# A post-LN decoder layer on one core: the gated attention stage with fp32 scores on 32-row groups, turned values and new orders

## The chip, the cores and the metric

One Trainium2 chip, one of its cores. The time is the device time of one launch in microseconds, as the median of several runs. Engines: TensorE (PE in the profile, PEld for its weight loads), VectorE (DVE), ScalarE (ACT), GpSimd (POOL) and SyncE (SP), which issues the transfers. The program is written instruction by instruction: each engine has its own list and runs it in order, and the lists are tied by semaphores.

## What is computed

Eight sequences of 128 tokens and 256 channels run through three sublayers, each followed by a layer norm of x + f(x).

```
x = layernorm(x + attention(x, Wq, Wk, Wv, Wo))      # 16 heads of 128, 4 key groups, RoPE
x = layernorm(x + convmix(ctx, ctx, x, kernel, D))   # long convolution of k*v, times x
x = layernorm(x + gated(x, W_gate, W_qkv))

def gated(x):
    gating = softmax(x @ W_gate.T)                   # 16 heads
    indicator, top1 = one_hot(argmax(gating)), max(gating)
    q, k, v = split(x @ W_qkv.T)                     # each 16 heads of 16
    k_shared = sum_h indicator * k                   # one key of 16 for a token
    v_shared = sum_h indicator * top1 * v
    att = softmax(causal(q_h . k_shared / sqrt(16)))
    return concat_h(att @ v_shared)
```

## The kernel before

**Phase a** (to about 248 us) does the first attention and the convolution. **The last stage**, here called the stage, does the rest of the second sublayer and the whole third one, batch by batch (b = 0 to 7, one batch is 128 tokens). Work that belongs to different batches is interleaved. For a batch b it is, with the functions of the code:

1. `first_apply` (VectorE) normalises x[b] with the statistics of the first layer norm into the buffer `x1[j]` (j = b mod 2). `x1_turn` (TensorE) transposes it, `mix_query` (ScalarE) copies it to `qmix`.
2. `products` (GpSimd, in the halves NEAR and FAR, 15 products of 128x32 to 128x256) multiplies the convolved pairs with it, `mix_sum` (VectorE, 128x2048 to 128x256) sums, `mix_turn` transposes back, `add_mix` adds. `norm_stats`, `norm_aggr`, `norm_eps` (VectorE), `second_power` (GpSimd, the power of -1/2) and `second_apply` (VectorE, into `x2[j]`) are the second layer norm. `keep_x2` (ScalarE) copies it to x[b].
3. `x2_turn` and `x2_copy` transpose it. `gate_project`, `kv_project` (two fp32 matmuls with 512 columns) and `query_project` (four with 128 columns) project. `gate_copy`, `gating` and `gate_exp` choose one head a token. `share` (VectorE) masks keys and values, sums them, repeats the shared key eight times into `krep` and scales the value into `vext` (128x17, the last column 1).
4. Scores: `query_hi` and `query_lo` write the fp32 queries as two fp32r parts, high and low, one below the other on 64 and 64 partitions (`qf`). `key_turn` transposes `krep`, `key_copy` copies it twice, and `block_keys_hi` (ScalarE) and `block_keys` (GpSimd) multiply the high and low parts with a 0/1 column per head (`blocks`) into `kblock`, 128x512. `fscores(b, j, c)` makes the scores of chunk c (four heads, 128x512) in one bank: two fp32r matmuls, then a bf16 matmul of the identity with the causal mask.
5. For each chunk: `frow_max` (VectorE, L1283), `fexps` (ScalarE, four exponentials of 128x128), `fturn` (four transposes, L625), `fprob_copy`, and `fvalues` (L636), which holds the transposed probabilities as weights and streams the 17 columns of `vext`, a head at a time.
6. `y_invert`, `y_scale` and `add_ffn` (VectorE) divide by the sums and add x[b] in `ynorm`, then the third layer norm ends in `norm_apply` (VectorE) into x[b] and a store from SP's queue (L342).

On each engine the order of the stage is written by hand: a prologue, then `seq(b, j)` for batches 0 to 3 and `last_seq` for 4 to 7 (`phase_b`). Score banks and transposed-probability banks are two each; the maxima share `neg_max` (two sets). An fp32 matmul appears in the trace as two records, each with a weight load; the fp32r and bf16 ones as one. L1208 is `norm_apply` for both norms, L1494 the power, L1255 `query_lo`, L1278 the scaling into `vext`, L1305 `add_ffn`, L1487 the last product of `block_keys`, L1294 `y_invert`, L596 `query_project`, L584 `kv_project`, L576 `gate_project`, L568, L550 and L560 the turns of x2, x1 and mix, L1093 the accumulation of the first attention's output, L1275 the copy into `krep`, L300 and L303 `products`.

## Time and profile before

| | us |
|---|---|
| median of 3 runs | 372.49 (372.28 to 373.48) |
| profiled execution | 370.43 |
| its span (first to last instruction) | 368.5 |
| mean granted TensorE clock | 0.968 |
| busy: TensorE, VectorE, ScalarE, GpSimd | 325.6, 274.5, 226.3, 207.5 |

The profile is one execution. The busy time of TensorE is modelled, since matmuls are pipelined: a record's duration includes latency that a stream hides, and its cost in a stream is the distance from one start to the next. The chain of waits gives these distances. "x8" is a group of eight records. Line numbers are those of the code above.

### The profile page before, as it was taken

What the parts mean: (1) busy time and instruction counts of PE and PEld (TensorE: products, weight loads), DVE (VectorE), ACT (ScalarE), POOL (GpSimd) and SP (SyncE); (2) the same over time, 40 slices, a digit from 0 to 9 for tenths busy, and PEclk for the clock granted to TensorE, in tenths of its full rate; (3) what the DMA queues carried; (4) which work ended last, traced back from release to release, by engine and by line L of the source; (5) the groups of instructions that cost most, each with busy time, mean ns of one, the idle gap of its engine ahead of it and who ended that gap; (6) DMA issues with size and microseconds to landing.
All of it is one profiled execution on the core that took longest, in us unless ns stands there. A gap on an engine that the chain in (4) does not pass through costs nothing.

```text
span 368.5 us, 5868 instructions
## 1 busy us (share of the span) xinstructions
PE 325.6 (88%) x1912; PEld 257.9 (70%) x1912; DVE 274.5 (74%) x527; ACT 226.3 (61%) x703; POOL 207.5 (56%) x291
## 2 busy tenths in 40 slices
PE   1958899999999999999999999673889999999993
PEld 0745778788778788778788788552477767777783
DVE  2774966955966955966955956988889999998662
ACT  4548567666567666667666655322467687688772
POOL 0488654756754756753756752885948767822200
PEclk9989999999999999999999999997789999999996
DMA  7911000031010031000040000000000000000000
GB/s 258 343 54 57 4 28 2 1 116 57 1 30 0 3 114 59 1 28 2 0 126 0 2 2 0 3 0 0 0 4 0 16 14 1 18 16 14 0 16 28
DMA packets 5757, 13.05 MB, mean 35 GB/s; under 512 B 992, under 2 KB 3168, under 8 KB 5472
## 3 DMA queue, kind: packets, MB, share of 16 engines
q1 hardware_dynamic: 5184, 11.90, 9.5%
q10 hardware_dynamic: 544, 0.79, 0.7%
q8 instruction: 15, 0.25, 0.2%
q14 instruction: 14, 0.11, 0.1%
HBM read 11.63 MB, written 1.05 MB: 34 GB/s over the span
## 4 chain that ended last, share of the span: by engine, by line
PE 61%; DVE 25%; issue 8%; ACT 2%; POOL 2%; DMA 1%; POOLq 0%; DVEq 0%; ACTq 0%
PE bank L357 13%; PE bank L478 12%; PE bank L388 8%; PE bank L374 7%; PE bank L467 5%; PE bank L456 3%; DVE toep L1029 3%; PE bank L636 3%; DVE t_cos L1219 2%; DVE neg_max L1283 2%; DMA x_raw<-in_xt 1%; PE bank L625 1%; PE bank L584 1%; DVE t_cos L996 1%; DVE v_tok L1208 1%
## 5 line engine op out<-in xcount | busy, mean ns | idle before, releaser
L1431 POOL TENSOR_TENSOR prob<-prob,rden 128x512 f32<-128x512 f32 x32 | 33.5, 1047 | 72.3 <-DVE rden L1056 72.3
L1410 POOL TENSOR_TENSOR t_sin<-rot,sin 128x512 f32<-128x512 f32 x40 | 54.3, 1359 | 27.4 <-ACT rot L752 24.7
L776 ACT ACTIVATE prob<-bank,neg_max 128x128 f32<-128x128 f32 x128 | 45.4, 368 | 39.2 <-DVE neg_max L1049 39.1
L357 PE MATMUL bank<-x_hi,w_hi 128*128 128x512 f32 x96 | 37.2, 470 | 8.6 <-ACT w_hi L733 8.1
L912 ACT ACTIVATE prob<-bank,neg_max 128x128 f32<-128x128 f32 x128 | 36.8, 375 | 11.7 <-DVE neg_max L1283 11.3
L388 PEld LDWEIGHTS bank<-k_rope,q_rope 128*128 128x128 f32 x256 | 34.6, 198 | 10.3 <-DVE q_rope L1009 4.9
L478 PE MATMUL bank<-wo_hi,head_hi 128*128 128x256 f32 x128 | 39.0, 304 | 3.0 <-DVE head_lo L1083 3.0
L388 PE MATMUL bank<-k_rope,q_rope 128*128 128x128 f32 x256 | 35.1, 282 | 4.5 <-DVE q_rope L1009 4.5
L300 POOL TENSOR_TENSOR q_rope<-y,rot 128x128 f32<-128x128 f32 (+7 forms) x60 | 31.4, 530 | 10.2 <-ACT rot L862 10.2
L478 PE MATMUL bank<-wo_lo,head_hi 128*128 128x256 f32 x128 | 36.1, 282 | 0.0
L478 PE MATMUL bank<-wo_hi,head_lo 128*128 128x256 f32 x128 | 36.1, 282 | 0.0
L636 PEld LDWEIGHTS bank<-vext,probT 128*128 128x128 f32 x256 | 33.2, 198 | 3.1 <-issue 2.9
L1400 POOL TENSOR_TENSOR kv<-ctxT 128x256 f32<-128x256 f32 (+3 forms) x64 | 35.3, 585 | 0.0
L374 PE MATMUL bank<-kv,toep 128*128 128x288 f32 x96 | 29.1, 414 | 5.8 <-DVE t_cos L996 5.8
L751 ACT COPY rot<-bank 64x512 f32<-64x512 f32 x40 | 23.4, 584 | 17.3 <-PE bank L357 16.4
L1083 DVE TENSOR_TENSOR head_lo<-bank,head_hi 128x512 fp32r<-128x512 f32 x32 | 21.9, 686 | 15.4 <-ACT head_hi L816 15.4
L467 PE MATMUL bank<-probT,v_tok 128*128 128x512 f32 x64 | 33.2, 600 | 0.0
L1494 POOL TENSOR_TENSOR rstd<-var_eps,half_pow 128x1 f32<-128x1 f32 (+1 forms) x18 | 11.6, 644 | 37.8 <-DVE var_eps L1203 36.8
L636 PE MATMUL bank<-vext,probT 128*128 128x17 f32 x256 | 32.0, 258 | 0.0
L357 PE MATMUL bank<-x_hi,w_lo 128*128 128x512 f32 x96 | 30.9, 403 | 0.0
L1009 DVE TENSOR_TENSOR q_rope<-t_cos,t_sin 128x512 f32<-128x512 f32 x32 | 30.0, 941 | 1.1
L357 PE MATMUL bank<-x_lo,w_hi 128*128 128x512 f32 x96 | 30.8, 402 | 0.0
(106 smaller groups left out, 813.5 us busy)
## 6 DMA issues: line engine op xcount, KB each, us to landing
w_raw<-in_wqkv SPq DMA_DIRECT2D x3, 768.0 KB, 4.9
toep<-in_toep SPq DMA_DIRECT2D x8, 256.0 KB, 3.2
wo_raw<-in_wo SPq DMA_DIRECT2D x4, 512.0 KB, 3.5
x_raw<-in_xt SPq DMA_DIRECT2D x2, 512.0 KB, 6.1
ctxT<-in_ctx SPq DMA_DIRECT2D x1, 1024.0 KB, 9.0
x<-in_x SPq DMA_DIRECT2D x1, 1024.0 KB, 10.2
out<-x SPq DMA_DIRECT2D x8, 128.0 KB, 1.7
wf<-in_wf SPq DMA_DIRECT2D x1, 784.0 KB, 4.6
```

The costliest lines, as they stand in the source:

```text
L300: last = eng.tensor_tensor(pr[:, :, d * HD:d * HD + (n - 1) * (HD + 1) + 1:HD + 1], y[:, :, at:at + n], q[:, :, 0:n], ALU.mult)
L357: last = pe.matmul(out[:, :], wp[:, c, col:col + P], xp[:, j, c, :], start=(c + n == 0), stop=(c == C - 1 and n == 2))
L374: last = pe.matmul(out, toep[:, j, hh, tap:tap + P], kv[:, j, m, hh * NB:(hh + 1) * NB, :], start=(m == 0), stop=(m == lb))
L388: last = pe.matmul(score_bank[k % 2][:, h * P:(h + 1) * P], q_rope[:, j, h, k * P:(k + 1) * P], k_rope[:, j, k * P:(k + 1) * P], start=Tru ...
L467: pe.matmul(headT_bank[:, :], v_tok[:, j, k * P:(k + 1) * P], probT[:, k % 2, :], start=True, stop=True).then_inc(pv_done, 1)
L478: last = pe.matmul(acc_bank[k // 2][:, (k % 2) * D:(k % 2 + 1) * D], hp[:, k % 2, h * P:(h + 1) * P], wp[:, 4 * v + h, :], start=(h + n == ...
L636: last = pe.matmul(y_bank[:, f * (FD + 1):(f + 1) * (FD + 1)], probT[:, c % 2, h * P:(h + 1) * P], vext[:, b, :], start=True, stop=True)
L776: last = act.activation(prob[:, k % 2, h * P:(h + 1) * P], score_bank[k % 2][:, h * P:(h + 1) * P], ACT.Exp, bias=neg_max[:, k % 2, h:h + ...
L912: last = act.activation(prob[:, c % 2, h * P:(h + 1) * P], fscore_bank[c % 2][:, h * P:(h + 1) * P], ACT.Exp, bias=neg_max[:, c % 2, h:h + 1])
L1400: last = pool.tensor_tensor(kv[:, buf, :, :, at:at + n], src[:, :, :, 0:n], src[:, :, :, d:HD], ALU.mult)
L1410: pool.tensor_tensor(t_sin[:, par, :].rearrange("p (b t) -> p b t", b=BH), rot[:, par, :].rearrange("p (b t) -> p b t", b=BH), sin[:, :].u ...
L1431: pool.tensor_tensor(own, own, rden[:, k % 2, :].unsqueeze(2).to_broadcast([P, HG, P]), ALU.mult).then_inc(norm_done, 1)
```

## The change

Only the last stage and what feeds it change. The scores are fp32 matmuls on a group of 32 rows per chunk (two heads of 16 for each half of the 256 output columns), and the chunks are issued in pairs, alternately. The mask comes first. `krep` is laid out with zeros between the copies, so that its transpose is already the block pattern: two key transposes and one copy give `kblock`, 128x256. `query_hi`, `query_lo`, `block_keys`, `block_keys_hi` and the input `blocks` go; the rows of the query weights are permuted to suit. Three score banks rotate; the transposed probabilities have one bank. `fvalues` holds `vext` (now 32 wide, filled with zeros) as weights on a group of 32 columns per head and streams the probabilities; its result is transposed, so `yT_copy` (ScalarE) and `y_turn` (four fp32 transposes into the bank of the keys and values) are new. `x1` and `x2` go: x[b] is normalised and added to in place, and `keep_x2` goes. The scaling into `vext` moves from VectorE to ScalarE (`values_in`), `add_ffn` from VectorE to GpSimd; `ynorm` has two buffers. `phase_b` goes: every engine has one `seq(i)` with conditions, in which the batches lie further apart (the third norm of batch i-2, the shares of i+1, the mix of i+2, the first norm of i+5).

```diff
-            def fscores(b, j, c):
-                if c == 0:
-                    pe.wait_ge(kblock_hi_done, b + 1)
-                    pe.wait_ge(kblock_lo_done, b + 1)
-                    pe.wait_ge(qf_lo_done, b + 1)
-                out = fscore_bank[c % 2]
-                pe.matmul(out[:, :], qf[:, j, c, :], kblock[:, j, 0, :, :], start=True, stop=False)
-                pe.matmul(out[:, :], qf[:, j, c, :], kblock[:, j, 1, :, :], start=False, stop=False)
-                pe.matmul(out[:, :].rearrange("p (h k) -> p h k", k=P), identb[:, :],
-                          causal[:, :].unsqueeze(1).to_broadcast([P, 4, P]),
-                          start=False, stop=True).then_inc(fscores_done, 1)
+            def fscores(b, j, pair):
+                if pair == 0:
+                    pe.wait_ge(kblock_done, b + 1)
+                if 4 * b + 2 * pair > 1:
+                    pe.wait_ge(fexp_done, 4 * b + 2 * pair - 1)
+                both = (2 * pair, 2 * pair + 1)
+                bank_of = [fscore_bank[(4 * b + c) % 3] for c in range(FC)]
+                for c in both:
+                    pe.matmul(bank_of[c][:, :].rearrange("p (h k) -> p h k", k=P), identb[:, :],
+                              causal[:, :].unsqueeze(1).to_broadcast([P, 4, P]), start=True, stop=False)
+                for n in range(C):
+                    for c in both:
+                        rows = slice(c * GROUP, (c + 1) * GROUP)
+                        last = pe.matmul(bank_of[c][:, n * D:(n + 1) * D], qf[rows, j, n, :],
+                                         kblock[rows, j, :], start=False, stop=(n == C - 1),
+                                         tile_position=(c * GROUP, 0))
+                        if n == C - 1:
+                            last.then_inc(fscores_done, 1)
...
 (fvalues)
-                    last = pe.matmul(y_bank[:, f * (FD + 1):(f + 1) * (FD + 1)],
-                                     probT[:, c % 2, h * P:(h + 1) * P], vext[:, b, :],
-                                     start=True, stop=True)
+                    last = pe.matmul(y_bank[h * YW:(h + 1) * YW, c * P:(c + 1) * P], vext[:, b, :],
+                                     probT[:, c % 2, h * P:(h + 1) * P], start=True, stop=True,
+                                     tile_position=(0, h * YW))
...
+            def y_turn(b):
+                pe.wait_ge(yT_copied, b + 1)
+                pe.wait_ge(masked_done, min(b + 3, NB))
+                at_least(pe, ynorm_done, b, 1)
+                for c in range(FC):
+                    last = pe.transpose(kvf_bank[:, c * P:(c + 1) * P], yT[:, c * P:(c + 1) * P],
+                                        ident[:, :])
+                last.then_inc(y_done, 1)
...
+            def seq(i):      # TensorE; each line only where its batch exists
+                fturn(i, 0); kv_project(i + 1, (i + 1) % 2, 1); query_project(i + 1, (i + 1) % 2)
+                fvalues(i - 1, 3); mix_turn(i + 2, i % 2); fturn(i, 1); key_turn(i + 1)
+                fvalues(i, 0); y_turn(i - 1); fscores(i + 1, (i + 1) % 2, 0); x2_turn(i + 2, i % 2)
+                fturn(i, 2); fvalues(i, 1); gate_project(i + 2, i % 2); x1_turn(i + 5, (i + 1) % 2)
+                kv_project(i + 2, i % 2, 0); fturn(i, 3); fvalues(i, 2); fscores(i + 1, (i + 1) % 2, 1)
...
+            def seq(i):      # ScalarE
+                x2_copy(i + 1); fprob_copy(i - 1, 2); fexps(i, 0); mix_query(i + 4); gate_copy(i + 1)
+                fprob_copy(i - 1, 3); fexps(i, 1); gate_exp(i + 1); fprob_copy(i, 0); fexps(i, 2)
+                query_copy(i + 1); yT_copy(i - 1); values_in(i + 1); key_copy(i + 1)
+                fprob_copy(i, 1); fexps(i, 3)
...
+            def seq(i):      # VectorE
+                y_invert(i - 2); y_scale(i - 2); second_apply(i + 1); norm_apply(1, ln3, i - 3)
+                frow_max(i, 0); frow_max(i, 1); mix_sum(i + 2); gating(i + 1); frow_max(i, 2)
+                norm_stats, norm_aggr, norm_eps (1, ln3, i - 2); share(i + 1)
+                add_mix(i + 2); norm_stats, norm_aggr, norm_eps (0, ln2, i + 2)
+                frow_max(i, 3); first_apply(i + 5)
...
+            def seq(i):      # GpSimd
+                add_ffn(i); products(i + 5, (i + 1) % 2, NEAR); products(i + 5, (i + 1) % 2, FAR)
+                power(rstd_of[1][:, :], var_eps_of[1][:, :], ln3, i + 1); second_power(i + 4)
```

The four orders above are written on fewer lines than in the code, where each call stands under its own condition. The prologues change with them: VectorE does `share(0)` before the mix of batch 1 and `first_stats(1)`, `first_apply(4)` behind the first two row maxima, TensorE turns x1 of batch 3 before the first keys, and GpSimd does the products of batches 2, 3 and 4 ahead of its loop.

## Rows read from the trace of the kernel before

**Rows 1.** The page, busy time by engine.

```profile
PE 325.6 (88%) x1912; PEld 257.9 (70%) x1912; DVE 274.5 (74%) x527; ACT 226.3 (61%) x703; POOL 207.5 (56%) x291
```

**Rows 2.** Table by stretches: busy us of each engine, clock.

```profile
250.00:262.00 12.00, 6.35 (x18) 3.74 (x19) 8.95 (x30) 5.01 (x18) 7.40 (x16) 0.61 0.00 0
...
288.00:301.00 13.00, 12.36 (x84) 9.40 (x83) 12.65 (x32) 9.79 (x35) 9.48 (x20) 1.00 0.03 11
```

**Rows 3.** VectorE alone in order of time: start, us, what.

```profile
299.77 0.69 DVE L1283 TENSOR_REDUCE neg_max<-bank 128x4 f32<-128x512 f32 x1
...
306.22 0.42 DVE L1278 TENSOR_SCALAR vext<-kv_shared,gprob 128x16 f32<-128x16 f32 x1
306.55 0.68 DVE L1283 TENSOR_REDUCE neg_max<-bank 128x4 f32<-128x512 f32 x1
...
308.67 0.42 DVE L1305 TENSOR_TENSOR x_raw<-x_raw,x 128x256 f32<-128x256 f32 x1
...
310.17 1.02 DVE L1208 TENSOR_SCALAR v_tok<-v_tok,mean_var,rstd 128x256 f32<-128x256 f32 x1
...
311.29 0.86 DVE L1255 SCALAR_TENSOR_TENSOR w_hi<-bank,w_hi 64x256 fp32r<-64x256 f32 x2
312.18 0.41 DVE L1208 TENSOR_SCALAR x<-x_raw,mean_var,rstd 128x256 f32<-128x256 f32 x1
...
312.94 0.69 DVE L1283 TENSOR_REDUCE neg_max<-bank 128x4 f32<-128x512 f32 x1
```

**Rows 4.** Chain in order of time: start, us, what; then one line's durations.

```profile
351.54 0.80 PE bank L636 x8
352.34 0.48 PE bank L625 x4
352.82 0.23 PE bank L615
...
L625 PE MATMUL bank<-ident,prob x128: 272/273/421, 263.7 to 360.6; 128*128 128x128 f32 x128
```

**Rows 5.** The same chain, TensorE's other work.

```profile
272.01 0.43 PE bank L568 x2
...
280.08 0.22 PE bank L560 x2
...
339.36 0.35 PE bank L576 x4
...
341.78 1.73 PE bank L584 x4
...
347.16 1.00 PE bank L596 x8
```

**Rows 6.** VectorE alone in the batches 4 to 7.

```profile
334.71 0.26 DVE L1294 RECIPROCAL yden<-bank 128x16 f32<-128x16 f32 x1
...
339.39 0.69 DVE L1283 TENSOR_REDUCE neg_max<-bank 128x4 f32<-128x512 f32 x1 [0.39 <-PE bank L617]
...
347.20 0.26 DVE L1294 RECIPROCAL yden<-bank 128x16 f32<-128x16 f32 x1
...
351.58 0.69 DVE L1283 TENSOR_REDUCE neg_max<-bank 128x4 f32<-128x512 f32 x1 [0.27 <-PE bank L617]
```

**Rows 7.** GpSimd's products and the VectorE copy, in order of time.

```profile
300.81 1.38 POOL L300 TENSOR_TENSOR q_rope<-y,rot 128x256 f32<-128x256 f32 x2 [2.11 <-ACT rot L862]
...
310.00 1.04 POOL L1487 TENSOR_TENSOR x_hi<-ksT_lo,blocks 128x512 fp32r<-128x512 f32 x1
...
265.63 2.15 DVE L1275 COPY x_raw<-kv_shared 128x128 f32<-128x128 f32 x1
```

**Rows 8.** Start of the last stage in order of time.

```profile
247.07 1.88 PE L584 MATMUL bank<-wf,k_rope 128*128 128x512 f32 x4
247.27 0.69 DVE L1093 TENSOR_TENSOR x<-bank,x 128x512 f32<-128x512 f32 x1 [0.20 <-PE bank L478]
```

**Rows 9.** End of the span in order of time.

```profile
365.97 0.41 DVE L1208 TENSOR_SCALAR x<-x_raw,mean_var,rstd 128x256 f32<-128x256 f32 x1 [0.66 <-POOL rstd L1494]
```

More of the change, by code:

```diff
@@ L88, in decoder_kernel @@
         causal = sb("causal", [P, P], BF16)
-        blocks = sb("blocks", [P, FC])
         ties = sb("ties", [P, FH])
@@ new lines, in key_turn @@
+                for e in range(2):
+                    last = pe.transpose(tf_bank[:, e * P:(e + 1) * P], krep[:, e * P:(e + 1) * P], ident[:, :])
+                last.then_inc(ksT_done, 1)
+            def fscores(b, j, pair):
[16 more added lines that the diff above has]
+                            last.then_inc(fscores_done, 1)
@@ L719, in _ @@
+            for i in range(NB + 1):
+                seq(i)
         @block.scalar
@@ L989, in _ @@
+            for i in range(NB + 1):
+                seq(i)
         @block.vector
@@ L1012, in _ @@
             dve.memset(half_pow[:, :], -0.5)
+            dve.memset(krep[:, :], 0.0)
+            dve.memset(vext[:, :, FD + 1:YW], 0.0)
             dve.memset(vext[:, :, FD:FD + 1], 1.0).then_inc(const_set, 1)
@@ L1247, in gating @@
                                   ).then_inc(chosen_done, 1)
[L1249 to L1258 removed]
+            kz = krep[:, :].rearrange("p (n x) -> p n x", x=P + FD)[:, :, 0:P].rearrange(
+                "p n (g x) -> p n g x", x=2 * FD)[:, :, :, 0:FD]
             def share(b):
@@ L1387, in _ @@
-            phase_b(dve, seq, last_seq)
-            norm_apply(1, ln3, NB - 1, y_flat, x[:, NB - 1, :])
+            first_stats(1)
+            first_apply(4, 0)
+            def seq(i):
+                if 0 <= i - 2 < NB:
+                    y_invert(i - 2)
+                    y_scale(i - 2)
+                if 1 <= i + 1 < NB:
+                    second_apply(i + 1, (i + 1) % 2)
+                if 0 <= i - 3 < NB:
+                    norm_apply(1, ln3, i - 3, y_flat(i - 3), x[:, i - 3, :])
+                if 1 <= i < NB:
+                    frow_max(i, 0)
+                    frow_max(i, 1)
+                if 2 <= i + 2 < NB:
+                    mix_sum(i + 2, i % 2)
+                if 1 <= i + 1 < NB:
+                    gating(i + 1)
+                if 0 <= i < NB:
+                    frow_max(i, 2)
+                if 0 <= i - 2 < NB:
+                    norm_stats(1, ln3, i - 2, y_flat(i - 2))
+                    norm_aggr(1, ln3, i - 2)
+                    norm_eps(1, ln3, i - 2)
+                if 1 <= i + 1 < NB:
+                    share(i + 1)
+                if 2 <= i + 2 < NB:
+                    add_mix(i + 2, i % 2)
+                    norm_stats(0, ln2, i + 2, x[:, i + 2, :])
+                    norm_aggr(0, ln2, i + 2)
+                    norm_eps(0, ln2, i + 2)
+                if 0 <= i < NB:
+                    frow_max(i, 3)
+                if 5 <= i + 5 < NB:
+                    first_apply(i + 5, (i + 1) % 2)
@@ L1390, in _ @@
+            for i in range(NB + 3):
+                seq(i)
         @block.gpsimd
```

485 lines of the change are left out of this document (168 added, 317 removed).

## The prediction

> **What bounds the kernel now.** The page comes first: TensorE is busy 88% of the span, VectorE 74% [rows 1]. These are averages, so the second view is the table by stretches. In the last stage one batch takes about 13 us, and in such a stretch TensorE is busy 12.4 of 13 us, VectorE 12.65, ScalarE 9.8 and GpSimd 9.5 [rows 2]: two engines are full at once. The third view, VectorE alone in order of time, says which ends last. From one `frow_max` at 299.77 to the same one at 312.94 is a round of 13.17 us with no idle time in it [rows 3], and the chain of waits in this stretch names only VectorE. So for the batches 0 to 3 VectorE sets the pace. How near TensorE is behind it: one chunk costs it 0.80 (values, 8 records), 0.48 (four transposes) and 3 x 0.235 (scores), 1.98 us [rows 4], and a batch has four, 7.9. To that come keys and values 1.73, queries 1.00, gate 0.35, the turns of x1, mix and x2 at 0.22 to 0.43, 0.87 together, and the key turn, 0.1 [rows 5]: 12.0 us of a round of 13.17. Once the mix sums have gone (batches 4 to 7) VectorE has gaps and TensorE sets the pace: the reciprocals of batches 4 and 5 lie at 334.71 and 347.20, 12.5 us apart, where TensorE's work by the same rows is 11.6, so it ran 0.9 above its own sum. The row maxima of chunk 0 of batches 6 and 7 lie at 339.39 and 351.58 [rows 6].
>
> **The change, VectorE.** Removed in each round: `query_lo`, from 311.29 to 312.18, 0.89; `add_ffn`, 0.42; the scaling into `vext`, 306.22 to 306.55, 0.33 [rows 3]. The second normalisation (`second_apply`) took 1.02 us there, and the same form takes 0.41 at 312.18. Beneath the long one lies GpSimd's `kblock` product of 1.04 us, begun 0.17 earlier and ended 0.15 before it [rows 3, 7]; this product goes, and with it 0.6. Together 2.3 us. What is added: the two normalisations are no longer threaded into each other, so statistics, aggregate, eps and the pair `y_invert`, `y_scale` follow each other directly, which I estimate at 0.05 to 0.1 for each of some five steps, 0.4. The third normalisation now stands right behind the release of `add_ffn` on GpSimd. A VectorE copy that stood under GpSimd's products took 2.15 us once, though it is smaller than the 128x256 form that takes 0.41 [rows 3, 7]. The bounds of this collision are 0 and the residual of one GpSimd product of 128x256, 0.7 (half of 1.38 [rows 7]); I take 0.4, since the start times are nearly equal. Writing x in place instead of through x1 and x2 is nothing for VectorE. Sum: 13.17 - 2.3 + 0.4 + 0.4 = 11.7 us, with bounds 11.3 and 12.4. The Trainium skill (SBUF — State Buffer, Who interferes with whom) says that copies and tensor_scalar in a two-port mode, and VectorE instructions with two SBUF inputs, share a port pair with GpSimd and that whichever starts first blocks the other fully. The 1.02 and 2.15 us rows agree. By it the moved add is a VectorE instruction that could collide and no longer does.
>
> **ScalarE and GpSimd** have one answer: ScalarE loses four masking activations, one of two query copies, one of two key copies and `keep_x2`, and gains one 128x512 copy (`yT_copy`) and a small activation, so it falls below its 9.8 of 13 [rows 2]. GpSimd loses 1.5 us (`block_keys`) and gains one add of 128x256, 0.7 by the product of that shape [rows 7], so it stays below 9.5. The add has no other price until the tail, where nothing hides it. What is queued behind its wait for `ynorm` on GpSimd is the products of batch i+5, whose result is needed two rounds later, so that wait delays nobody. The 2 KB load of `blocks` goes from SP's queue; it lands long before the stage, worth nothing. SP's eight stores keep their place.
>
> **TensorE.** The trace has no matmul on row or column groups, so their overlap must be bounded from both sides. An fp32 matmul is two records. With 512 columns four records take 1.73, 0.43 each [rows 5]; 256 columns are then 0.215 a record, 128 columns 0.11. Scores: a pair of chunks has two masks (2 x 0.235) and four fp32 matmuls, eight records of 0.215. In series that is 0.47 + 1.72 = 2.19 a pair, 4.4 a batch. If a record may run beside the one before it only where that stands on another row group, which is every second one, then five slots are left: 0.47 + 1.08, 3.1 a batch. If both chunks overlap in full, 2.7. Before, it was 2.8. Values: eight records of 0.11 on four column groups, 0.88 a chunk in series, 0.55 with every second one beside its neighbour, 0.3 at best; a batch 3.5, 2.2 or 1.2, against 3.2 before [rows 4]. New besides: the turn back, four transposes, 0.48 [rows 4], and a second key transpose, 0.12. Left as they are: transposes of the probabilities 1.92, keys and values 1.73, queries 1.00, gate 0.35, three turns 0.87, first key transpose 0.12. The middle case is 3.1 + 2.2 + 0.48 + 0.12 + 5.99 = 11.9 us a round, with all in series 14.5, with all beside each other 10.5. I take the middle: the reason for issuing two chunks alternately is that neighbours stand on different groups, and only every second record does.
>
> **Why the round is longer than either sum.** VectorE 11.7 and TensorE 11.9 would each be full and wait for the other in turn. There is also a ring: scores of chunk 0, row maxima, mix sum, gating, maximum of chunk 2, `share`, key turn, key copy, scores of the next batch. Its VectorE part is 7.9 us by start-to-start times of such instructions, then 0.4 for the turn, 0.5 for the copy, up to 1.0 in which TensorE does `fvalues` and `y_turn` in between, and 1.6 for the first pair: 11.4. All three are within 0.5 of one another. Where TensorE set the pace before, it ran 0.9 above its sum [rows 6]; where VectorE did, nothing. I take 0.6 on 11.9: T = 12.5 us a round instead of 13.17.
>
> **From the round to the end.** Start of the stage: the last accumulation is at 247.27, the last keys' matmul of batch 0 runs till about 249 [rows 8]. From there the new order by durations of rows gives: krep(0) 250.9, scores of pair 0 till 254.0, eps of batch 1 at 255.9, rstd for batches 4 to 7 at 260.5, second normalisation of batch 1 at 261.4 (TensorE idles in front of its turn and runs at the lower clock, as it did before with a granted 0.61 between 250 and 262 [rows 2]), mix sum of batch 2 till 263.6, scores of pair 1 till 267.3, row maximum of chunk 0 of batch 1 at 273.5. Then that of batch 6 is at 273.5 + 5T, that of batch 7 one T less 1 later (no mix sum, no next keys), and the tail 17.2 behind it. The tail: 0.7 maximum, 8.0 of ScalarE's exponentials and copies, then transposes 0.66, copy 0.62, values 0.75, `yT_copy` 0.65, turn back 0.66, invert 0.3, scale 0.45, GpSimd add 0.85, the four steps of the norm 1.5, apply 0.45, and 2.1 from there to the end of the span, as from 365.97 to 368.5 less the apply [rows 9]. Before it is 368.5 - 351.58 = 16.9 [rows 6]; the copy, the turn and the add lengthen it by what the shorter values give back. End = 289.7 + 6T = 364.7 us at T = 12.5, 3.8 below the span of 368.5. The profiled execution took 370.43, 1.93 more than its span, and the median of the runs is 372.49, another 2.06 more; I carry the difference over: 368.7 us. The equation breaks even at T = 13.13.
>
> **Rivals.** *Changing between the whole array and groups costs a drain (slower).* A transpose of the probabilities lasts 0.273 in its row but the next one follows 0.12 behind [rows 4], so 0.15 of each is latency that a stream hides. A batch has twelve changes (four around the two score pairs, eight around the values). Some four stand where TensorE waits for a copy anyway; eight at 0.15 are 1.2, T = 13.7, span 371.9, median 375.9. It decides against the change from 0.08 us a change upwards. For it: nothing in the trace shows a change without price. Against: the bf16 mask matmul between fp32 ones costs its 0.235 and no more [rows 4], though that is a change of type alone. The Trainium skill states this rule (TensorEngine Tiling, Key Properties): changing the tiling mode drains TensorE, changing only the tile doesn't. No row here shows it.
>
> *The groups do not overlap.* TensorE needs 14.5, T = 15.1, span 380.3, median 384.3. For it: the two records of one matmul share a group. The Trainium skill (TensorE: Matmul & The Clock Gate, Packing small matmuls) speaks against it, with 3.07 times the rate for four row groups; no run here shows that either.
>
> *The groups overlap in full.* TensorE 10.5, VectorE alone sets T = 11.6 to 11.7, span 359.6, median 363.6.
>
> *Nothing comes of it:* a drain of half that price or more collisions on VectorE, T = 12.9 to 13.3, within 0.3% (about what a measurement of this kernel can tell from no change).
>
> **How the numbers follow.** Forecast 0.50 (T from 11.9 to 12.9, 365.1 to 371.1), full overlap 0.12, nothing 0.12, drains 0.14, series 0.12. Faster by over 0.3%: 0.50 + 0.12 = 0.62; same 0.12; slower 0.26. The range leaves out series and half of full overlap, 0.18: 362.5 to 377.5.
>
> **What would show it.** Records on line of `fscores`: if the starts of neighbours are 0.215 apart everywhere, series; if every second start falls on the one before, the middle. `fvalues` under 0.6 a chunk. Gaps of 0.1 or more in front of the first record after a change of groups: drains. The VectorE round from `frow_max` to `frow_max` near 12.5, with `second_apply` back at 0.4. The row maximum of batch 7 near 347.5 and 17.2 us behind it. I am wrong if the start of the stage is later by over 3 us, if a VectorE copy is held under a whole run of GpSimd products in each round, or if the clock falls below 1.0 in the rounds because TensorE idles more.

## The result and the profile after

The changed kernel takes 362.79 us (median of 4 runs, 361.88 to 364.21) against 372.38 us for the kernel before in the same comparison (4 runs, 371.22 to 373.48): ratio 0.9746, 95% interval 0.970 to 0.979. The forecast was 368.7 us. The time lies in the range that the prediction gave, but the gain, 9.6 us by medians and 6.9 us by the spans of the two profiled executions, is far larger than the 3.8 us of the forecast.

| | before | after |
|---|---|---|
| profiled execution, its span | 370.43, 368.5 | 363.41, 361.6 |
| granted TensorE clock, mean | 0.968 | 0.969 |
| busy TensorE, VectorE, ScalarE, GpSimd | 325.6, 274.5, 226.3, 207.5 | 317.1, 260.7, 217.8, 201.2 |
| one round (`y_invert` of one batch to the next), batches 1 to 3 | 13.18, 13.19 | 11.33, 11.31 |

Line numbers of after: L601 the mask, L606 `fscores`, L617 `fturn`, L627 `fvalues`, L639 `y_turn`, L563 `gate_project`, L572 `kv_project`, L581 `query_project`, L589 `key_turn`, L555, L547 and L537 the turns of x2, mix and x1, L1163 `norm_apply` (both norms), L1227 `frow_max`, L1173 `mix_sum`, L1239 `y_invert`, L1392 the residual add on GpSimd. The page, where [rows 1] answers:

```profile
PE 317.1 (88%) x2016; PEld 237.7 (66%) x2016; DVE 260.7 (72%) x497; ACT 217.8 (60%) x663; POOL 201.2 (56%) x283
```

The table by stretches (as [rows 2]: length, busy us and records of TensorE, its weight loads, VectorE, ScalarE, GpSimd, then granted clock):

```profile
250.00:262.00 12.00, 3.68 (x25) 2.19 (x23) 9.42 (x23) 2.48 (x8) 7.29 (x17) 0.80 0.00 0
...
308.00:319.00 11.00, 11.00 (x94) 7.00 (x93) 10.68 (x25) 8.47 (x28) 8.80 (x18) 1.00 0.05 15
```

In such a stretch TensorE is busy all of 11.00 us and VectorE 10.68. The chain of waits of after in one round (start, us, what) has only TensorE in it, and no idle time. So it is from 298.5 to 344 us; in the two rounds before that the chain also goes through VectorE:

```profile
308.51 0.43 PE bank L601 x2
308.94 1.06 PE bank L606 x8
310.00 0.37 PE bank L555 x2
310.37 0.44 PE bank L617 x4
310.80 0.36 PE bank L627 x8
311.16 0.55 PE bank L563 x4
...
313.45 0.54 PE bank L601 x2
313.99 1.06 PE bank L606 x8
315.06 0.59 PE bank L617 x4
...
319.23 0.59 PE bank L639 x4
319.82 0.43 PE bank L601 x2
```

From 308.51 to 319.82 are 11.31 us: the round is TensorE's own sum, exactly. A pair's scores cost 1.06, a chunk's values 0.36 (before 0.80 [rows 4]). VectorE alone, in order of time, shows the steps of [rows 3], and the row maxima of batches 1, 4, 6 and 7:

```profile
275.10 1.27 DVE L1227 TENSOR_REDUCE fneg_max<-bank 128x4 f32<-128x512 f32 x2
...
297.46 0.25 DVE L1239 RECIPROCAL yden<-bank 128x16 f32<-128x16 f32 x1
...
308.79 0.25 DVE L1239 RECIPROCAL yden<-bank 128x16 f32<-128x16 f32 x1
...
309.41 0.41 DVE L1163 TENSOR_SCALAR x<-x,mean_var,rstd 128x256 f32<-128x256 f32 x1
309.73 0.82 DVE L1163 TENSOR_SCALAR x<-x_raw,mean_var,rstd 128x256 f32<-128x256 f32 x1
310.47 1.27 DVE L1227 TENSOR_REDUCE fneg_max<-bank 128x4 f32<-128x512 f32 x2
...
333.01 1.27 DVE L1227 TENSOR_REDUCE fneg_max<-bank 128x4 f32<-128x512 f32 x2
...
343.78 1.29 DVE L1227 TENSOR_REDUCE fneg_max<-bank 128x4 f32<-128x512 f32 x2 [0.45 <-PE bank L606]
```

The second normalisation is back at 0.41 from 1.02. The third takes 0.82: GpSimd's add runs from 309.57 to 310.40 beside it.

### The profile page after: what moved, and what is told of

It reads as the page before. It is cut to its first block, busy times and chain, and to the rows that moved or that the text cites. A ratio compares the mean times of both kernels' runs of the same rounds, so it can differ in the third digit from the quotient of the medians.

```text
span 361.6 us, 6079 instructions
## 1 busy us (share of the span) xinstructions
PE 317.1 (88%) x2016; PEld 237.7 (66%) x2016; DVE 260.7 (72%) x497; ACT 217.8 (60%) x663; POOL 201.2 (56%) x283
## 4 chain that ended last, share of the span: by engine, by line
PE 71%; DVE 15%; issue 5%; POOL 3%; DMA 2%; ACT 2%; SPq 1%; POOLq 0%; DVEq 0%; ACTq 0%
PE bank L465 12%; PE bank L344 12%; PE bank L375 8%; PE bank L361 7%; PE bank L454 6%; PE bank L572 4%; PE bank L606 4%; PE bank L617 4%; PE bank L443 4%; DVE toep L985 3%; PE bank L627 2%; DMA anti<-in_anti 2%; PE bank L601 2%; DVE t_cos L950 2%; PE bank L563 1%
## 5 line engine op out<-in xcount | busy, mean ns | idle before, releaser
L760 ACT ACTIVATE prob<-bank,neg_max 128x128 f32<-128x128 f32 x128 | 45.3, 367 | 39.2 <-DVE neg_max L1005 39.1
L883 ACT ACTIVATE prob<-bank,fneg_max 128x128 f32<-128x128 f32 x128 | 36.7, 378 | 6.5 <-DVE fneg_max L1227 6.5
L1397 POOL TENSOR_TENSOR rstd<-var_eps,half_pow 128x1 f32<-128x1 f32 (+1 forms) x18 | 10.8, 601 | 45.7 <-DVE var_eps L1158 44.7
L454 PE MATMUL bank<-probT,v_tok 128*128 128x512 f32 x64 | 34.0, 614 | 0.0
L950 DVE TENSOR_TENSOR t_cos<-bank,cos 128x512 f32<-128x512 f32 x40 | 27.2, 681 | 2.2 <-ACT rot L736 1.7
L465 PEld LDWEIGHTS bank<-wo_hi,head_hi 128*128 128x128 f32 x128 | 24.4, 191 | 5.5 <-DVE head_lo L1039 3.3
```

Source lines behind the costliest of these rows:

```text
L454: pe.matmul(headT_bank[:, :], v_tok[:, j, k * P:(k + 1) * P], probT[:, k % 2, :], start=True, stop=True).then_inc(pv_done, 1)
L465: last = pe.matmul(acc_bank[k // 2][:, (k % 2) * D:(k % 2 + 1) * D], hp[:, k % 2, h * P:(h + 1) * P], wp[:, 4 * v + h, :], start=(h + n == ...
L760: last = act.activation(prob[:, k % 2, h * P:(h + 1) * P], score_bank[k % 2][:, h * P:(h + 1) * P], ACT.Exp, bias=neg_max[:, k % 2, h:h + ...
L883: last = act.activation(prob[:, c % 2, h * P:(h + 1) * P], scored[:, h * P:(h + 1) * P], ACT.Exp, bias=fneg_max[:, c, h:h + 1])
L950: dve.tensor_tensor(t_cos[:, par, :].rearrange("p (b t) -> p b t", b=BH), bank_in[:, :].rearrange("p (b t) -> p b t", b=BH), cos[:, :].uns ...
```

## The experiments

Ratios are to runs of the kernel before, made beside it on the same chip. Rounds are the distances between the `y_invert` of successive batches. Phase a alone ends up to 3 us earlier or later from one execution to the next (in the changed kernel and its variants the `mix_sum` of batch 1 starts between 249.97 and 253.15 us), so mechanisms are read from intervals inside the stage and not from the ends of spans.

**Do the row groups overlap, and does the order matter?** First the order alone (`s_series`):

```diff
-                for n in range(C):
-                    for c in both:
+                for c in both:
+                    for n in range(C):
```

> Only the order of the four score matmuls of a pair is changed: both halves of one chunk, then both of the other, in place of alternately. If alternation is what makes neighbours run side by side, the eight records of a pair go from 1.06 us towards the series value of 1.72 (at most one overlap is left in the middle, 1.5 to 1.7), and since TensorE sets the round, the round goes from 11.3 to 12.2 to 12.6 us. If the records of one row group overlap anyway, or the 1.06 comes from something else (weight loads), both stay at 1.06 and 11.3.

Measured: 362.77 us (2 runs, ratio 0.976), rounds of 11.30 and 11.34. The chain of waits:

```profile
306.90 0.43 PE bank L601 x2
307.33 1.07 PE bank L606 x8
```

The alternation gives nothing. With that the reason that I had given for "every second record" is refuted, but not explained. Two more runs did that: `s_full` uses all 128 rows,

```diff
-                        last = pe.matmul(bank_of[c][:, n * D:(n + 1) * D], qf[rows, j, n, :],
-                                         kblock[rows, j, :], start=False, stop=(n == C - 1),
-                                         tile_position=(c * GROUP, 0))
+                        last = pe.matmul(bank_of[c][:, n * D:(n + 1) * D], qf[:, j, n, :],
+                                         kblock[:, j, :], start=False, stop=(n == C - 1))
```

> Of the changed kernel, the four fp32 matmuls of a pair of chunks' scores use all 128 rows instead of a group of 32 (each half of each chunk the same columns, 256 wide, the masks as before); the sums then mix the chunks, so the scores are other numbers. The question is where 0.107 us for a record of 256 columns comes from. Theory A (a record of 32 rows is a smaller operation and streams, or loads its weights, faster than one on the whole array, whose 512 columns take 0.43, so 0.215 for 256): eight records take 1.72 us, less one or two changes of group at 0.15 each, so the pair is 0.5 longer and a round 11.31 + 1.0 = 12.3. Theory B (the cost of a record goes by its columns and fixed parts, and 0.43 for 512 columns is limited by something else; the group of rows has no part in it): eight records stay at 0.8 to 1.06, and the round falls by the eliminated changes, two a pair, to 10.9 to 11.3. Transposes and masks around them should lose their extra 0.10 to 0.15 behind the scores in both.

and `s_one` issues everything on one group of 32 rows:

```diff
-                        rows = slice(c * GROUP, (c + 1) * GROUP)
+                        rows = slice(0, GROUP)
...
-                                         tile_position=(c * GROUP, 0))
+                                         tile_position=(0, 0))
```

> Of the changed kernel, all scores of a pair of chunks are issued on row group 0 (rows 0 to 31 of the queries and keys for every chunk), so every chunk's scores are those of chunk 0. Nothing can stand beside its neighbour on another group. Theory A (a record of 32 rows takes half of one on the whole array by itself): eight records stay at 1.06 to 1.07 us and the round at 11.3. Theory B (the half comes from two groups in use, in whatever order): eight records take 1.7 to 1.9 us and the round 12.3 to 12.9. In between (1.2 to 1.6) would mean part of each.

One execution of each: 369.05 us and 377.9 us. The one run of the kernel before beside `s_one` took 380.3 us at a mean clock of 0.935, so the totals are not compared, only the intervals. The chain of `s_full`:

```profile
310.13 0.43 PE bank L601 x2
310.57 1.73 PE bank L605 x8
312.29 0.22 PE bank L555 x2
```

and that of `s_one`:

```profile
303.11 0.43 PE bank L601 x2
303.55 1.92 PE bank L606 x8
305.46 0.37 PE bank L555 x2
```

`s_full`: 0.215 a record, and the turn of x2 behind it takes 0.22. `s_one`: 1.92, which is eight times 0.215 and 0.20, and the turn takes 0.37. So a record of 32 rows is no faster than one of 128 (theory A of `s_one` falls); what halves the cost is that two groups are in use, and the pair costs 8 x 0.107 + 0.20 whichever order they come in. The rounds follow: 12.10 to 12.25 us in `s_full` (forecast 12.3), 12.8 to 13.1 in `s_one`. For `s_full` its theory A gave the right number with a wrong reason, since it had not separated rows from overlap. The Trainium skill (TensorE: Matmul & The Clock Gate, Why this matters for your kernels) says that one matmul of 32 rows lasts as long as one of 128 and that the gain is concurrency between tiles; these two runs agree. How four records of one group and then four of the next come to overlap as well as alternating ones stays open.

**Column groups** (`v_series`): all heads of `fvalues` on one group of 32 columns.

```diff
-                    last = pe.matmul(y_bank[h * YW:(h + 1) * YW, c * P:(c + 1) * P], vext[:, b, :],
+                    last = pe.matmul(y_bank[0:YW, c * P:(c + 1) * P], vext[:, b, :],
...
-                                     tile_position=(0, h * YW))
+                                     tile_position=(0, 0))
```

> All four heads of a chunk use column group 0 and write the same 32 rows, so only the last head's values survive in each chunk (heads are left out of the result; the work is the same). If the 0.36 us of a chunk's eight records comes from four column groups running together, it goes to the series value 0.8 to 0.9 and the round from 11.3 to about 13.1. If it comes from the narrow weights (32 columns) alone, it stays near 0.36.

Measured: 379.8 us (2 runs, ratio 1.021), rounds of 13.92 and 13.75. The chain:

```profile
317.33 0.99 PE bank L627 x8
318.32 0.55 PE bank L563 x4
```

0.99 is 8 x 0.107 + 0.13; with four groups it is 0.36, 8 x 0.027 + 0.14. So four column groups overlap in full, if the part beside the records is the same in both. The expected 0.8 to 0.9 and 13.1 us were too low: they had left out the price of the change, and 4 x 0.63 on 11.31 is 13.8.

**What does a change between whole array and groups cost?** A dummy matmul of 16 bf16 columns on the whole array, once behind the masks, where no change is added (`d_ahead`), once between the halves of the scores, where it adds two changes a pair (`d_between`, shown; in `d_ahead` the same matmul stands ahead of the loop):

```diff
+                    if n == 1:
+                        pe.matmul(bank_of[2 * pair][:, 0:16], identb[:, :], causal[:, 0:16], start=False, stop=False)
```

> Control for the next kernel: one more bf16 matmul of 16 columns on the whole array for each pair of chunks, right behind the masks, so no change between whole array and row groups is added. Cost: under 0.1 us a pair, the round 11.3 to 11.5.

> The same small matmul, but between the first and the second half of the pair's score matmuls, so each pair has two more changes between row groups and the whole array, four in a batch. If a change costs the 0.10 to 0.15 us that stands behind groups in the trace, the round is 0.4 to 0.7 us longer than that of the control. If changes are free, the two are equal within 0.1.

`d_ahead`: 362.75 us (2 runs), rounds of 11.34 and 11.31, a pair's scores 1.06: the dummy by itself is free. `d_between`: 367.25 us (2 runs, ratio 0.989), rounds of 11.71 to 11.85. Its chain:

```profile
311.04 0.63 PE bank L608 x4
311.67 0.12 PE bank L605
311.78 0.63 PE bank L608 x4
```

1.38 instead of 1.06 for two changes, 0.15 each; the rounds are 0.37 to 0.61 longer than those of `d_ahead` for four, 0.09 to 0.15 each. In after the same price shows wherever a whole-array group stands behind scores or values: transposes 0.59 instead of 0.44, the gate 0.55 instead of 0.35 [rows 5], a pair of masks 0.54 instead of 0.43. The Trainium skill's rule (TensorEngine Tiling, Key Properties) that a change of tiling mode drains TensorE and a change of tile alone doesn't agrees: 0.15 for the one, nothing visible for the other in `s_series`.

**The old values in the new order** (`v_old`): transposed probabilities as weights again, 17 columns streamed, no turn back, the division one round earlier.

```diff
-                    last = pe.matmul(y_bank[h * YW:(h + 1) * YW, c * P:(c + 1) * P], vext[:, b, :],
-                                     probT[:, c % 2, h * P:(h + 1) * P], start=True, stop=True,
-                                     tile_position=(0, h * YW))
+                    last = pe.matmul(y_bank[:, f * (FD + 1):(f + 1) * (FD + 1)],
+                                     probT[:, c % 2, h * P:(h + 1) * P], vext[:, b, 0:FD + 1],
+                                     start=True, stop=True)
```

> Undo one part: values as before (probabilities as weights, 17 columns streamed), no turn back, no copy for it; the division then stands one round earlier on VectorE. If TensorE sets the round, each round pays 4 x 0.80 in place of 4 x 0.36 and saves the turn of 0.59 and some changes of group, near 0.5 to 0.8: 11.3 + 1.76 - 0.59 - 0.6 = 11.9 us, and the end gives back about 1.2 us (copy and turn are gone from the tail). Total 2 to 4 us above the changed kernel. If VectorE sets the round, it stays at 11.3 and the total falls by the tail.

Measured: 427.69 us (4 runs, ratio 1.150, 1.140 to 1.160). Neither theory had this. The table by stretches:

```profile
275.00:286.00 11.00, 10.27 (x78) 7.82 (x74) 6.97 (x13) 6.89 (x24) 6.44 (x15) 1.00 0.00 1
286.00:297.00 11.00, 9.42 (x42) 7.14 (x43) 8.85 (x18) 4.77 (x15) 8.19 (x17) 0.63 0.01 1
297.00:308.00 11.00, 9.32 (x63) 7.33 (x61) 5.12 (x18) 5.10 (x16) 0.69 (x3) 0.90 0.00 0
308.00:319.00 11.00, 10.33 (x46) 7.99 (x44) 7.10 (x11) 5.51 (x19) 8.10 (x17) 0.56 0.04 13
330.00:345.00 15.00, 15.00 (x59) 10.53 (x59) 7.17 (x14) 5.99 (x20) 8.20 (x17) 0.50 0.03 9
```

TensorE waits 1.7 us for `krep` at 285.9, and from there to 405 us the granted clock is between 0.50 (the 1.2 GHz level all the time) and 0.90, in most stretches 0.50 to 0.66, though TensorE is busy 85 to 100% of each; at the lower level a pair's scores take 2.00 instead of 1.06. The edit also moves a wait: on VectorE the division of batch i-1 now stands in front of `share`, and the chain goes through both at 327 to 329 us. This run can't price the values at full clock. It does show that this order with the old values falls to the lower level and comes back from it only in part.

**Was VectorE the pace before, and what came next?** From the kernel before, the causal mask left out (`nomask_before`, and again with more runs as `nomask_again`), and 0.9 us of VectorE work left out (`light_before`):

```diff
-                pe.matmul(out[:, :], qf[:, j, c, :], kblock[:, j, 1, :, :], start=False, stop=False)
-                pe.matmul(out[:, :].rearrange("p (h k) -> p h k", k=P), identb[:, :],
-                          causal[:, :].unsqueeze(1).to_broadcast([P, 4, P]),
-                          start=False, stop=True).then_inc(fscores_done, 1)
+                pe.matmul(out[:, :], qf[:, j, c, :], kblock[:, j, 1, :, :], start=False, stop=True
+                          ).then_inc(fscores_done, 1)
```

> The kernel before with its causal mask matmuls left out (the scores are not masked). TensorE loses 4 x 0.235 = 0.94 us a batch. If VectorE sets the rounds of batches 0 to 3 there, they stay at 13.17 us and only the batches 4 to 7 gain, up to 0.9 each, 3 us in all. If TensorE sets them, the rounds fall to about 12.3 and the total by 6 to 7 us.

> The kernel before without the bf16 matmul that adds the causal mask (so the softmax sees all keys), once more, with several timed runs. If the loss of some 7 us of its first look belongs to the kernel, because TensorE with 0.94 us less work a batch waits more for VectorE and the granted clock falls below 1.00 in the rounds: ratio to the kernel before 1.01 to 1.02, granted clock 0.7 to 0.85 somewhere between 275 and 330. If it was one execution: ratio 0.995 to 1.00, since VectorE sets the pace in the rounds with mix sums, or 0.985 if TensorE gains in batches 4 to 7.

```diff
-                for r in range(2):
+                for r in range(1):
...
-                dve.tensor_tensor(y_flat, y_flat, x[:, b, :],
-                                  ALU.add).then_inc(ln3[0], 1)
```

> The kernel before with VectorE work left out: one of the two instructions of query_lo and the residual add of the last sublayer. VectorE loses 0.43 + 0.46 = 0.9 us a batch. If VectorE sets the rounds there, they fall from 13.17 to 12.3, where TensorE's sum of 12.0 is next. If TensorE runs 0.6 to 0.9 above its sum when it sets the pace, as I assumed, the round stops at 12.6 to 12.9.

`nomask_before` took 378.45 us (2 runs, ratio 1.018, 1.010 to 1.026), with 0.94 us less TensorE work a batch; a stretch of it:

```profile
301.00:316.00 15.00, 14.96 (x73) 12.11 (x73) 10.39 (x26) 8.45 (x30) 7.81 (x17) 0.66 0.03 9
```

The clock is 0.66 where before has 1.00, and the round is 17.3 us; neither expectation had this. In `nomask_again` three of four executions took 378.0 to 382.4 us at a mean clock of 0.92 to 0.93, and one took 371.2 at 0.956, as long as the kernel before beside it (median 371.45). So five of six executions ran at the lower clock and one did not: it is no single accident, and no fixed price of the edit either. The question about VectorE's pace was not answered by these two. `light_before` answered it: 371.64 us (8 runs, ratio 0.996, 0.991 to 1.002), and its rounds of 12.72 (285.03 to 297.75) and 12.81 (312.19 to 325.00), both at a clock of 1.00, stand against 13.18 before:

```profile
285.03 0.26 DVE L1295 RECIPROCAL yden<-bank 128x16 f32<-128x16 f32 x1
...
297.75 0.26 DVE L1295 RECIPROCAL yden<-bank 128x16 f32<-128x16 f32 x1
```

VectorE did set the pace; behind it stood 12.7 us, 0.7 above TensorE's sum of 12.0. The total shows none of it: the stretch from 275 to 286 us had a clock of 0.76 and the round between the two one of 0.88 (14.44 us). The chain of waits also shows what these 12.7 us are: not TensorE alone but a ring through three engines, from the exponentials of one batch to those of the next. In the turn from 284.5 to 297.2 us some 5.2 us of it are ScalarE's, among them 1.17 of `block_keys_hi` and 0.63 of `query_hi`, which the change removes; about 4.2 are TensorE's and 2.6 VectorE's.

**And in after?** The masks left out (`nomask_after`), and the residual add back on VectorE (`add_dve`):

```diff
-                for c in both:
-                    pe.matmul(bank_of[c][:, :].rearrange("p (h k) -> p h k", k=P), identb[:, :],
-                              causal[:, :].unsqueeze(1).to_broadcast([P, 4, P]), start=True, stop=False)
...
-                                         kblock[rows, j, :], start=False, stop=(n == C - 1),
+                                         kblock[rows, j, :], start=True, stop=True,
```

> The changed kernel with its causal mask matmuls left out (the scores are not masked). TensorE loses 1.0 to 1.1 us a round and one change of group. If TensorE alone sets the round of 11.3 us, it falls until VectorE stops it, whose own round by the start-to-start times is 10.8 to 11.0: T = 10.8 to 11.0. If VectorE already sets it, T stays at 11.3. If TensorE has no second behind it, T = 10.2.

```diff
+                    dve.wait_ge(ynorm_done, i - 1)
+                    dve.tensor_tensor(y_flat(i - 2), y_flat(i - 2), x[:, i - 2, :], ALU.add).then_inc(ln3[0], 1)
...
-                if 0 <= i < NB:
-                    add_ffn(i)
```

> Undo one part: the residual add of the last sublayer back on VectorE, in front of the third norm's statistics. VectorE gets 0.45 us a round more. With the masks left out VectorE alone set a round near 10.9, so 0.45 more makes 11.3 to 11.4: if TensorE sets the round of 11.3, it stays within 0.1, and the tail gets 0.4 shorter (0.42 on VectorE in place of 0.82 on GpSimd). If VectorE sets it, 11.75 and a total 2.5 us longer.

`nomask_after`: 361.76 us (2 runs), rounds of 10.95 at full clock instead of 11.31, with only VectorE, and short gaps between its instructions, in the chain: the next limit lies only 0.36 below.

```profile
309.98 0.25 DVE L1236 RECIPROCAL yden<-bank 128x16 f32<-128x16 f32 x1
...
320.92 0.25 DVE L1236 RECIPROCAL yden<-bank 128x16 f32<-128x16 f32 x1
```

`add_dve`: one execution, 366.62 us, rounds of 12.84, 11.95, 11.61, 11.51 and 11.26, where after has 11.66, 11.33, 11.31, 11.22 and 10.97. The add on VectorE costs 1.2 us in the first round, 0.6 in the second and 0.3 in the others, 2.7 in all: neither "within 0.1" nor 0.45 in each, though the sum is near the 2.5 of the second expectation.

**A better version.** In after TensorE waits 7.27 us for the second normalisation of batch 1 at the start of the stage (TensorE in order of time):

```profile
262.23 0.69 PE L555 MATMUL bank<-ident,x 128*128 128x128 f32 x2 [7.27 <-DVE x L1163]
```

`start` puts what this turn and the next keys need first on VectorE and GpSimd; the first normalisation of batch 4 on VectorE, its turn on TensorE and its copy on ScalarE move back:

```diff
             frow_max(0, 1)
+            second_apply(1, 1)
+            mix_sum(2, 0)
+            gating(1)
             first_stats(1)
-            first_apply(4, 0)
...
             products(2, 0, NEAR)
+            products(2, 0, FAR)
             second_power(1)
-            products(2, 0, FAR)
+            products(3, 1, NEAR)
             power(rstd1[:, BH:NB], var_eps1[:, BH:NB], ln1, 2)
-            products(3, 1, NEAR)
```

`start_tail` adds two edits for the end, the copy of batch 6's turned values and the residual add of batch 7 on VectorE (the copy isn't shown); `start_add` has only the add:

```diff
+                if i - 2 == NB - 1:
+                    dve.wait_ge(ynorm_done, NB)
+                    dve.tensor_tensor(y_flat(i - 2), y_flat(i - 2), x[:, i - 2, :], ALU.add).then_inc(ln3[0], 1)
...
-                if 0 <= i < NB:
+                if 0 <= i < NB - 1:
```

> A new start of the stage: the second normalisation of batch 1, its mix sum of batch 2 and gating come before the statistics for batches 4 to 7, GpSimd finishes the products of batch 2 ahead of the power it waits for, and the first x1 turn of batch 4 moves behind the first projections. In the changed kernel TensorE stands still for 7.3 us before the turn of x2 of batch 1 at 262.23. This turn can start at 258, and the rounds all follow 4 to 5 us earlier: total 358 to 359 us. If the start is not on the path (the stage is bound by the rounds alone from some later batch on), nothing changes.

> The same, and in the tail the copy of batch 6's turned values and the residual add of batch 7 on VectorE, which is idle there. The chain of waits of the changed kernel goes through that copy at 349.84 (0.76 of waiting on ScalarE) and the add at 356.74 (0.82 in place of 0.42): 1.0 to 1.4 us less than start.

> The changed kernel itself, as the base for the two others of this call: 362.8 us, round 11.3.

These three gave, of 6 runs each, 362.65 for after (ratio 0.981, 0.976 to 0.985), 360.76 for `start` (0.974, 0.970 to 0.977) and 359.59 for `start_tail` (0.972, 0.968 to 0.976). The median of `start` misses its expectation of 358 to 359 us by 1.8. Inside the trace the edit does what was expected: TensorE waits 2.91 us instead of 7.27, and from the row maximum of batch 0 to that of batch 1 are 14.9 us (258.38 to 273.29) instead of 18.9; but in this execution the row maximum of batch 0 itself came 2.2 us later than in after.

```profile
260.04 0.69 PE L555 MATMUL bank<-ident,x 128*128 128x128 f32 x2 [2.91 <-DVE x L1166]
```

By medians the tail's expectation of 1.0 to 1.4 was met. But the intervals inside the two profiles said otherwise: from the row maximum of batch 7 to the last division `start` has 12.16 us, `start_tail` 12.98, since the row maximum of chunk 2 waits behind the moved copy:

```profile
344.27 0.69 DVE L1285 COPY vT<-bank 128x512 f32<-128x512 f32 x1 [3.67 <-PE bank L627]
```

Hence three more:

> The new start alone, once more, beside the two versions of the tail. Theory A: within 0.3 us of the version with both edits, or faster by up to 0.5. Theory B: slower than it by 1.0 to 1.4. Row maximum of batch 7 to the last division 12.16, from there to the end 5.73.

> The new start with both edits of the tail (copy of the last turned values and last add on VectorE), once more. Theory A: row maximum of batch 7 to the last division 12.98, from there to the end 5.40, so 0.5 more than the new start; its median equals that of the new start or lies up to 0.5 above it. Theory B: its median is again 1.0 to 1.4 below.

> The new start, and of the two edits of the tail only one: VectorE instead of GpSimd adds x[b] for the last batch; the copy of the turned values stays on ScalarE. Theory A (the profile's intervals decide: the add on VectorE saves two hand-overs and 0.4, the moved copy costs 1.6 at the row maximum of chunk 2 and gives part of it back later): from the last division to the end of the span 5.40 instead of 5.73, from the row maximum of batch 7 to that division 12.16 as in start; so 0.3 faster than start, and 0.3 to 0.9 faster than with both edits. Theory B (the median of the run with both edits decides): slower than both edits by 0.5 to 1.0.

| 6 runs each | median | ratio | batch 7's row maximum to last division | to the end |
|---|---|---|---|---|
| `start_again` | 359.53 | 0.967 (0.963 to 0.971) | 12.17 | 5.70 |
| `start_tail_again` | 359.17 | 0.968 (0.964 to 0.973) | 12.75 | 5.44 |
| `start_add` | 358.92 | 0.966 (0.963 to 0.970) | 12.17 | 5.44 |

VectorE in order of time, `start_add`:

```profile
338.79 1.29 DVE L1230 TENSOR_REDUCE fneg_max<-bank 128x4 f32<-128x512 f32 x2 [0.45 <-PE bank L606]
...
342.76 0.69 DVE L1230 TENSOR_REDUCE fneg_max<-bank 128x4 f32<-128x512 f32 x1 [2.69 <-PE bank L606]
...
350.96 0.26 DVE L1242 RECIPROCAL yden<-bank 128x16 f32<-128x16 f32 x1 [1.80 <-PE bank L639]
```

Theory A held in the intervals: the moved copy costs 0.6 us here (0.8 the first time) and the moved add gives 0.26. Of its bounds for the medians it missed one narrowly: `start_again` came out 0.36 above `start_tail_again`, where 0.3 was allowed; theory B wanted 1.0 to 1.4. In the first two profiled executions the row maximum of batch 0 lay 2.45 us apart (258.38 and 255.93), more than the 1.2 us between their medians; that the medians differed for that reason is likely and not shown. The medians of the three can't tell them apart (their intervals overlap); the intervals of the trace do. `start_add`, 358.92 us, is the version I would keep: 3.4% faster than before.

## Why the prediction was right or wrong

By spans the forecast was 364.7 and the result 361.6, 3.1 lower. The pieces: the row maximum of batch 1 at 275.10 instead of 273.5 (+1.6); from there to that of batch 6 at 333.01, 57.91 us instead of 62.5 (-4.6); to that of batch 7 at 343.78, 10.77 instead of 11.5 (-0.7); the tail 17.8 instead of 17.2 (+0.6).

**VectorE's round: right in its terms, 0.8 too high in its sum.** It was forecast at 11.7, with a lower bound of 11.3; `nomask_after` shows 10.95. `second_apply` came back to 0.41, the third normalisation's collision is 0.41 where I took 0.4, and the unthreaded norms cost the 0.4 that I estimated. What remains is in the start-to-start times of `nomask_after` (311.67 to 322.61) against [rows 3]: 0.44 is `first_apply`, which in the new order runs for batch i+5 and so has ended before these rounds, and 0.3 are shorter steps at `chosen`, `gscore` and `krep`; why these are shorter is open. The stated upper bound of 12.4 doesn't follow from the stated terms either; they give 12.0.

**TensorE's sum, "every second record": the wrong step.** I took 11.9 and measured 11.31. For the scores I had five slots of 0.215, 1.08, and measured 1.06, which looks like a hit and isn't: it is full overlap, 0.86, and 0.20 for the changes. For the values the same two errors don't cancel: 0.55 forecast, 0.36 measured. Set out in the terms of the sum, the round from 308.51 to 319.82 is: scores and masks 2.6 instead of 3.1, values 0.9 instead of 2.2, changes of group 2.1 instead of nothing, the rest 5.8 instead of 6.6. So full overlap took off 1.8, the changes put 2.1 on, and the two errors cancelled, which is luck. The 0.6 by which the sum was too high lies in the rest: the turn of x1 isn't in these rounds (0.22), the turn of x2 was taken at 0.43 from a row at the lower clock [rows 5] and is 0.22, and transposes and queries are 0.3 shorter. `s_series`, `s_one` and `v_series` refute the middle case; the rival of full overlap had the mechanism right, and I had given it 0.12.

**The drains rival: right in price and count, wrong in consequence.** I had named 0.15 a change and twelve changes, of which I charged eight. `d_between` gives 0.12 to 0.15. If the rows without a change in front of them (transposes 0.44, masks 0.43, gate 0.35, two-record turns 0.22, scores 0.86, values 0.22) stand for the work itself, a round is 9.25 us of work and 2.06 more, nearly all of it changes, 0.16 for each of twelve. I had treated overlap and drains as alternatives with a chance each; they are two terms of one sum. The rival's break-even of 0.08 us a change was reckoned on top of the middle case and so was wrong too.

**"0.6 for waiting for each other": the other wrong step.** I carried a measured 0.9 of the old order into the new one. `light_before` confirms it for the old order, 0.7 above TensorE's sum. In the new kernel it is 0.0: from 298.5 to 344 us nothing stands in the chain but TensorE. That the wait is gone is shown; what took it away is not. Putting the batches further apart may have done it, or the 1.8 us of ScalarE's work that left the ring of `light_before`; the order wasn't tried apart from the other parts with the clock at 1.00.

Sum and waiting make 12.5 into 11.31; the forecast said T from 11.9 to 12.9. The first two of the five rounds behind 57.91 us were longer by the row maxima, 11.65 and 12.40: `first_apply` is still in them, and the third norm enters in front of the row maximum in the second.

**The start: +1.6.** The second normalisation of batch 1 came at 261.41, forecast 261.4, but the sum of the mix behind it ended 0.8 later than forecast and TensorE then ran 262 to 275 at a granted 0.79, where the first two records of the keys and values of batch 1 take 1.71 instead of 0.86 (the other two, at 269.18, are back at 0.87). The idle time stood in my account; the doubled durations behind it were costed too low.

**The tail: +0.6.** All of its steps were there, and 0.5 of the 0.6 is arithmetic: the terms that the prediction lists add up to 17.7, not 17.2, and 17.8 was measured. The transposes and the values of its last chunks are strung on ScalarE's exponentials and copies. `start_tail` shows that moving the copy to the idle engine makes it worse.

**The median.** I added the 2.06 us by which the median of before lay above its profiled execution. In after that difference is -0.6. Of the 5.9 us between forecast and median, 2.7 come from this term. It was mostly the chance of which execution was profiled: beside five other groups of runs the kernel before had medians of 370.4 to 372.2, on average 1.0 above the profiled 370.43, not 2.06.

## What to carry to other kernels

Here two groups of rows overlapped in full in both orders of issue and four groups of columns in the one that was tried, and a change between whole array and groups cost about 0.15 us: count both, as terms of one sum, and put group work together. A wait measured in one order of the program, with one set of engines in its ring, is not to be carried over to another; read which step ends last in the new one. Two wrong terms can cancel in a sum that comes out near, so check it term by term. A kernel whose stage reacts to a few us of chance in front of it is compared by intervals inside the trace, not by medians a microsecond apart.

## What the runs showed of the hardware that was not expected

- One fp32 record of 256 columns costs 0.215 us on 128 rows, on 32 rows alone too (`s_full` 1.73, `s_one` 1.92 for eight), and 0.107 when two groups are in use; 128 columns on one column group cost 0.107, on four 0.027 (each worked out from eight records less 0.13 to 0.20 for the change).
- A kernel with less TensorE work ran at a lower clock. `nomask_before` leaves out 0.94 us of bf16 matmuls a batch and is 1.8% slower, with a granted clock of 0.66 to 0.89 from 262 to 330 us; of six executions of this kernel one escaped it and took as long as the kernel before. `light_before` had a round at 0.88. `v_old` fell towards the 1.2 GHz level after a wait of 1.7 us and had a clock of 0.50 to 0.90 for the next 120 us, though TensorE was busy 85 to 100% of each stretch. Before and after run these rounds at 1.00. What exactly decides it stays open.
